# First convolution scored as plain fp32 products from a folded code table, first expert routing inside its turns

## The chip, the cores and the metric

The kernel runs on one NeuronCore of one Trainium2 chip. The metric is the device time of one execution in microseconds (us); each kernel is timed in several runs. The profile is one further execution, read by the hardware profiler. Its engines are PE (TensorE), DVE (VectorE), ACT (ScalarE), POOL (GpSimd) and SP (SyncE, which here only issues DMAs).

## The reference, cut to what matters

Sixteen images of 64 channels and 16 x 16 places pass through four blocks, each a "convolution" and an expert stage. Only the first convolution and what the first expert stage needs before it starts are changed:

```python
x = x + _L0_conv_ref(_ln_c(x), proj_w, proj_b, emb)      # _ln_c: mean and variance over the 64 channels
t = t + _L0_ffn_ref(_ln_t(t), ...)                       # 8 experts, the 2 likeliest of each token

# _L0_conv_ref, one row zf per token, K = 1024 codes of 64 values
zp = jnp.einsum('bchw,oc->bohw', z, proj_w) + proj_b[None, :, None, None]
dist = (zf * zf).sum(-1, keepdims=True) - 2.0 * (zf @ emb.T) + (emb * emb).sum(-1)[None, :]
idx = jnp.argmin(dist, axis=1)
z_q = emb[idx]
```

The first convolution thus gives each of the 4096 tokens the code nearest to its projected, normalised features. The term in zf alone is the same for all codes, so both kernels look for the largest of 2 z.e - e.e.

## The kernel before, in words

The program is written out by hand for each engine; semaphores order the engines and each engine does its work in the order written. `X` holds all tokens, 32 tiles of 128 tokens x 64 channels. The first convolution (`c0_*`) goes through eight turns (`PAIRS`), each for two images, that is four tiles j = 0 to 3 (`PT`).

*Preparation.* `load_first` brings the identity, the first images, the code table twice side by side, the projection and small tables. PE turns the 8 x 128 codes over (L251), ACT squares them (L266), and PE sums the squares with a matrix of -1 (L258). A product in plain fp32 is avoided: ACT and DVE split twice the code table into three bf16 parts `codes_a`, `codes_b`, `codes_c` (L267 to L291), and DVE splits the norms in three bf16 rows (`norm_parts`, L284 to L289).

*One turn g.* PE turns the images' channels into tokens (`c0_xload`, L299); DVE copies them to X (L421) and takes mean and variance (L122, L125); POOL makes the reciprocal deviation (L131, L132); DVE subtracts and multiplies (L136, L137); PE turns the normalised tokens (`c0_normt`, L306); ACT copies them to `xf` (L380), which has a 65th row of ones for the bias; PE projects them (`c0_project`, L313). ACT and DVE split the projection into three bf16 parts in `xa` and `xb` (L387 to L392, L457, L462). All of this is for the next turn's tokens and lies between the current turn's scorings. For each tile, `c0_scores` (L327) makes 128 x 1024 scores in two of four PSUM banks, by eight bf16 products: two with the norm rows, six with the parts. DVE finds the maximum (L471, eight values) and its index (L475). POOL gathers the code rows from memory (L526, an indirect DMA) and adds them to X (L535) one turn later. The two pairs of PSUM banks alternate by tile, so PE may score tile j+2 only when DVE has searched tile j (`c0_read`); a turn's first scoring also waits for the third part of the split (`c0_z`). DVE's index search of tile j waits until the gather of the same tile of the turn before has landed, since it overwrites the indices.

*Passage into the first expert stage.* The expert stages work on four blocks of eight tiles. `ffn_*_routing` gives the steps of one block: statistics (L920, L927), normalising on POOL (L1090 to L1103), turning the tokens (L707), the gate's logits (L715), ranking (L937 to L946), hits, combination (L950 to L980), turning the weights (L727, ACT L862), after which SP writes the weights to memory and reads them back broadcast (L672, L668). Block 0's steps stand before and in turn 7 and behind it; behind it DVE also takes the statistics of block 1; then comes `barrier` 1, where all four engines drain and wait for one another, and then the stage's products (up L773, activation on ACT L892, down L778). Behind some waits `wait_apart` increments a semaphore that nobody waits for.

## Time and profile before

| What | us |
|---|---|
| Three timed runs, median (lowest to highest) | 1025.54 (1020.04 to 1026.93) |
| Profiled execution: span, first to last instruction | 1015.0 |
| Profiled execution: its own device time | not recorded beside the span |
| PE busy in the span | 852.3 (84%) |
| DVE busy | 524.8 (52%) |
| ACT busy | 424.0 (42%) |
| POOL busy | 415.5 (41%) |
| Mean granted TensorE clock | 0.861 |

### The profile page before, as it was taken

What the parts mean: (1) busy time and instruction counts of PE and PEld (TensorE: products, weight loads), DVE (VectorE), ACT (ScalarE), POOL (GpSimd) and SP (SyncE); (2) the same over time, 40 slices, a digit from 0 to 9 for tenths busy, and PEclk for the clock granted to TensorE, in tenths of its full rate; (3) what the DMA queues carried; (4) which work ended last, traced back from release to release, by engine and by line L of the source; (5) the groups of instructions that cost most, each with busy time, mean ns of one, the idle gap of its engine ahead of it and who ended that gap; (6) DMA issues with size and microseconds to landing.
All of it is one profiled execution on the core that took longest, in us unless ns stands there. A gap on an engine that the chain in (4) does not pass through costs nothing.

```text
span 1015.0 us, 16664 instructions
## 1 busy us (share of the span) xinstructions
PE 852.3 (84%) x5582; PEld 395.5 (39%) x5588; DVE 524.8 (52%) x1845; ACT 424.0 (42%) x777; POOL 415.5 (41%) x533
## 2 busy tenths in 40 slices
PE   4768676889588999987778789989899998998995
PEld 1222222222355666665222478423333224652221
DVE  6887854555234444454553354355656453434542
ACT  3212213556235455454444343344344333646662
POOL 0343443555333233232343781544453643014642
PEclk9987777999559789799587785899999999969997
DMA  9410003222000000000234000422232310002341
GB/s 181 79 25 9 8 6 85 89 85 85 1 1 2 2 2 2 1 3 2 74 111 153 1 2 0 134 67 86 68 94 83 91 56 1 2 2 84 120 113 62
DMA packets 48701, 52.57 MB, mean 52 GB/s; under 512 B 18838, under 2 KB 27178, under 8 KB 48618
## 3 DMA queue, kind: packets, MB, share of 16 engines
q1 hardware_dynamic: 47594, 50.46, 18.0%
q0 software_dynamic: 1024, 1.05, 0.6%
q8 instruction: 46, 0.75, 0.3%
q14 instruction: 37, 0.30, 0.1%
HBM read 49.78 MB, written 1.70 MB: 51 GB/s over the span
## 4 chain that ended last, share of the span: by engine, by line
PE 62%; DVE 15%; issue 8%; POOL 8%; ACT 6%; POOLq 0%; SPq 0%; DVEq 0%; another core or an unknown queue 0%; DMA 0%; ACTq 0%
PE ps L773 17%; PE ps L778 11%; PE ps L1273 6%; PE ps L327 3%; DVE best L471 3%; DVE code L475 3%; PE ps L1245 2%; PE ps L1318 2%; PE ps L1268 2%; POOL work L1147 2%; PE ps L1644 2%; PE ps L715 2%; PE ps L1664 2%; DVE work L1009 1%; ACT work L892 1%
## 5 line engine op out<-in xcount | busy, mean ns | idle before, releaser
L773 PE MATMUL ps<-xT,wall 64*128 64x512 f32 x576 | 170.7, 674 | 5.7 <-ACT work L892 3.3
L778 PE MATMUL ps<-work,down 128*64 128x512 f32 x576 | 165.2, 655 | 6.8 <-POOL work L1135 6.1
L892 ACT ACTIVATE work<-ps,b1t 128x512 f32<-128x512 f32 x160 | 100.3, 685 | 79.2 <-PE ps L773 79.1
L1009 DVE TENSOR_TENSOR work<-aq,ps 128x512 f32<-128x512 f32 x128 | 82.2, 684 | 97.3 <-PE ps L773 89.5
L1128 POOL TENSOR_TENSOR work<-xT,cwb 128x512 f32<-128x512 f32 x64 | 81.4, 1275 | 104.0 <-PE ps L773 78.6
L887 ACT ACTIVATE aq<-ps 128x512 f32<-128x512 f32 x128 | 69.4, 594 | 118.9 <-PE ps L773 118.8
L1147 POOL TENSOR_TENSOR work<-work 128x512 f32<-128x512 f32 x56 | 71.0, 1268 | 81.6 <-DVE work L1035 79.3
L773 PEld LDWEIGHTS ps<-xT,wall 64*128 64x128 f32 x576 | 53.8, 203 | 111.8 <-issue 105.5
L1035 DVE SCALAR_TENSOR_TENSOR work<-ps,b1t,cwb 128x512 f32<-128x512 f32 x64 | 47.9, 748 | 77.7 <-PE ps L778 66.9
L773 PE MATMUL ps<-work,wall 64*128 64x512 f32 x256 | 73.5, 650 | 9.9 <-DVE work L1009 5.3
L1457 DVE TENSOR_REDUCE maxr<-ps 128x4 f32<-128x640 f32 x32 | 26.4, 825 | 79.6 <-PE ps L1273 79.6
L778 PEld LDWEIGHTS ps<-work,down 128*64 128x64 f32 x576 | 29.9, 140 | 94.2 <-DVE work L1009 35.1
L526 POOL DMA_INDIRECT zq<-in_L_conv_emb_dram,code x32 | 31.6, 988 | 69.2 <-DVE code L475 63.6
L327 PE MATMUL ps<-mt,ak 128*128 128x512 bf16 x186 | 57.6, 450 | 0.6 <-issue 0.4
L1392 ACT ACTIVATE pt<-ps 128x864 f32<-128x864 f32 x32 | 28.5, 891 | 63.5 <-PE ps L1273 63.5
L1268 PE MATMUL ps<-sight 32*128 32x160 bf16 (+2 forms) x512 | 38.0, 255 | 14.8 <-ACT pt L1393 7.7
L471 DVE MAX8 best<-ps 128x8 f32<-128x1024 f32 x32 | 39.3, 1228 | 17.8 <-PE ps L327 15.5
L773 PEld LDWEIGHTS ps<-work,wall 64*128 64x128 f32 x256 | 20.0, 189 | 62.6 <-POOL work L1128 38.1
L1273 PE MATMUL ps<-ak,aq 32*128 32x160 f32 (+2 forms) x512 | 43.4, 388 | 0.0
L475 DVE FIND_INDEX8 code<-best,ps 128x8 uint32<-128x1024 f32 x32 | 39.1, 1223 | 0.0
L1090 POOL TENSOR_SCALAR fveps<-fmv 128x8 f32<-128x8 f32 x16 | 3.6, 224 | 84.6 <-DVE fmv L927 61.4
L327 PE MATMUL ps<-norm_parts,ones 3*128 3x512 bf16 x64 | 22.5, 437 | 18.6 <-DVE ak L462 15.4
(245 smaller groups left out, 1484.1 us busy)
## 6 DMA issues: line engine op xcount, KB each, us to landing
cwb<-weight_rows SPq DMA_DIRECT2D x320, 128.0 KB, 3.0
wall<-in_L_ffn_w_dram SPq DMA_DIRECT2D x4, 512.0 KB, 10.6
wall<-in_L_ffn_W_dram SPq DMA_DIRECT2D x4, 256.0 KB, 9.5
out_dram<-tokens SPq DMA_DIRECT2D x8, 128.0 KB, 1.7
tokens<-in_x_dram SPq DMA_DIRECT2D x1, 896.0 KB, 5.3
ak<-in_L_conv_emb_dram SPq DMA_DIRECT2D x2, 256.0 KB
down<-in_L_ffn_W_dram SPq DMA_DIRECT2D x2, 256.0 KB
down<-in_L_ffn_w_dram SPq DMA_DIRECT2D x1, 512.0 KB
```

Of the source, the lines that this page charges most:

```text
L327: ins = pe.matmul(m.ps[:, 2 * (j % 2) + k, :], z, codes[:, k * 512:(k + 1) * 512], start=(n == 0), stop=(n == len(passes) - 1))
L471: n = o.step(dve.max(m.best[:, j, :], sc))
L475: dve.max_index(m.code[:, j, :], m.best[:, j, :], sc).then_inc(s.c0_read, 1)
L773: ins = pe.matmul(m.ps[:, bank + half, :], m.wall[r, at + g * P:at + (g + 1) * P], x[r, :], start=True, stop=True)
L778: ins = pe.matmul(m.ps[half * C:half * C + C, bank, :], m.down[l][:, n % G, :], m.hid[:, n % 3, half, :], start=start, stop=True, skip_gro ...
L887: act.activation(m.silu[:, n % 2, half, :], m.ps[:, 4 * (n % 2) + half, :], ACT.Silu).then_inc(s.f_silu, 1)
L892: act.activation(m.hid[:, n % 3, half, :], m.ps[:, 2 * (n % 2) + half, :], ACT.Gelu, bias=bias)\
L1009: dve.tensor_tensor(m.hid[:, n % 3, half, :], m.silu[:, n % 2, half, :], m.ps[:, 2 + half, :], ALU.mult)\
L1128: pool.tensor_tensor(m.xs[:, n % 2, :], m.xT[:, n // G, :], slot, ALU.mult).then_inc(s.f_pw, 1)
L1147: pool.tensor_tensor(acc, acc, m.part[:, k % 2, :], ALU.add).then_inc(s.f_pw, 1)
L1268: pe.matmul(m.ps[:, h, at_of(g, h):at_of(g, h) + w], m.place[r, g, t * P:(t + 1) * P], m.unseen[r, g, lo:lo + w], start=True, stop=True)
L1273: ins = pe.matmul(m.ps[:, h, at_of(g, h):at_of(g, h) + w], fixed[r, i % RING, g, t * P:(t + 1) * P], moving[r, i % RING, g, lo:lo + w], st ...
```

## The change

In the preparation the projection W, b is folded into the code table. `lead` is a 128 x 128 matrix with W in its first 64 columns, b in the 65th, and -0.5 at its lower half's 65th column. Multiplied with the turned codes over their squares (`codes_in`), it gives 65 rows that matter: W'e, and b.e - e.e/2. Doubled, they are `codes`, in fp32. A tile's scores are then two fp32 products of `xf` (64 feature rows, a row of ones, 63 rows of zeros, in two alternating buffers) with the halves of `codes`. The projection of each turn, the split into bf16 parts and the norm rows go.

The copy into X moves from DVE to ACT (`arrive`), subtracting the mean and multiplying from DVE to POOL (`norm`). Block 0's routing of the first expert stage is placed in pieces: statistics in turn 3, POOL's part in turns 3 and 4, the preparing transposes in turn 5, tokens and logits in turn 6, ranking, hits and combination between the searches of turn 7. The barrier between the first convolution and the first expert stage goes; PE instead waits for the last search, and the statistics of block sb wait for their additions. The memset of `vals` moves from the start to just before the first search. `wait_apart` is not used in the first convolution any more.

```diff
+        (m.lead[0:C, 0:C], d.L0_conv_proj_w),
+        (m.lead[0:C, C:C + 1], d.L0_conv_proj_b.rearrange("(o a) -> o a", a=1)),
     ]
     for dst, src in loads:
         sp.dma_start(dst, src, allow_slow_non_contiguous=src.shape[-1] == 1).then_inc(s.ld_first, 16)
@@ -158,7 +133,7 @@
     sp.dma_start(m.xall[:, 1:PAIRS, :], x[:, 1:PAIRS, :]).then_inc(s.c0_rest_in, 16)
...
+def c0_pe_fold(pe, nc, m, s):
+
+    pe.wait_ge(s.lead_set, 1)
     pe.wait_ge(s.codes_sq, 1)
-    pe.wait_ge(s.ones_rows, 1)
     for k in range(2):
-        ins = pe.matmul(m.ps[0:3, 2 + k, :], m.minus_one[0:C, 0:3], m.codes_sq[:, k * 512:(k + 1) * 512],
-                        start=True, stop=True)
+        ins = pe.matmul(m.ps[:, 2 + k, :], m.lead[:, :], m.codes_in[:, k * 512:(k + 1) * 512], start=True, stop=True)
     ins.then_inc(s.codes_n, 1)
 
...
+    act.activation(m.codes_in[C:P, :], turned[C:P, :], ACT.Square)
+    act.wait_ge(s.codes_plain, 1)
+    act.activation(m.codes_in[0:C, 512:CODES], turned[0:C, 512:CODES], ACT.Copy).then_inc(s.codes_sq, 1)
+
+
+def c0_act_codes(act, nc, m, s):
+    act.wait_ge(s.codes_n, 1)
+    act.activation(m.codes[:, 512:CODES], m.ps[:, 3, :], ACT.Copy, scale=2.0).then_inc(s.codes_ready, 1)
...
+    dve.tensor_copy(m.codes_in[0:C, 0:512], turned[0:C, 0:512]).then_inc(s.codes_plain, 1)
...
+    dve.tensor_scalar(m.codes[:, 0:512], m.ps[:, 2, :], 2.0, None, ALU.mult).then_inc(s.codes_ready, 1)
...
+    if g > 0:
+        pe.wait_ge(s.c0_here, g)
...
+    if g > 0:
+        pe.wait_ge(s.c0_xf, g)
...
-def c0_project(pe, m, s, g):
-
-    pe.wait_ge(s.c0_xf, g + 1)
-    pe.matmul(m.ps[:, 4, :], m.proj0[:, :], m.xf[:, :], start=True, stop=True).then_inc(s.c0_zp, 1)
...
-        pe.wait_ge(s.c0_z, g + 1)
+        pe.wait_ge(s.c0_xf, g + 1)
...
-    passes = ((m.ones3[:, :], m.norm_parts), (za, m.codes_a), (za, m.codes_b), (zb, m.codes_c))
-    for n, (z, codes) in enumerate(passes):
-        for k in range(2):
-            ins = pe.matmul(m.ps[:, 2 * (j % 2) + k, :], z, codes[:, k * 512:(k + 1) * 512],
-                            start=(n == 0), stop=(n == len(passes) - 1))
+    for k in range(2):
+        ins = pe.matmul(m.ps[:, 2 * (j % 2) + k, :], m.xf[:, g % 2, j * P:(j + 1) * P],
+                        m.codes[:, k * 512:(k + 1) * 512], start=True, stop=True)
     ins.then_inc(s.c0_scored, 1)
...
     c0_normt(pe, m, s, 0)
-    c0_project(pe, m, s, 0)
-    pe.wait_ge(s.c0_rest, 1)
     c0_xload(pe, m, s, 1)
-    pe.wait_ge(s.codes_ready, 1)
-
...
+    pe.wait_ge(s.codes_ready, 2)
+    tokens, logits, weights = ffn_pe_routing(pe, m, s, 0)
+
+    for g in range(PAIRS):
+        c0_scores(pe, m, s, g, 0)
+        if g + 1 < PAIRS:
             c0_normt(pe, m, s, g + 1)
-        c0_scores(pe, m, s, g, 1, b)
-        if ahead > 0:
-            c0_project(pe, m, s, g + 1)
...
+        if g == PAIRS - 2:
+            pe.wait_ge(s.prepared, 1)
+            tokens(0)
+        c0_scores(pe, m, s, g, 1)
+        if g + 2 < PAIRS:
             c0_xload(pe, m, s, g + 2)
...
+        c0_scores(pe, m, s, g, 2)
+        if g == PAIRS - 3:
+            prepare_pe(pe, nc, m, s)
+        elif g == PAIRS - 2:
+            pe.wait_ge(s.ld_up, 16 * UP_LOADS)
+            logits(0)
+        c0_scores(pe, m, s, g, 3)
     weights(0)
+    pe.wait_ge(s.c0_read, PAIRS * PT + 2)
...
+    def arrive(g):
+        x = m.X[:, g * PT:(g + 1) * PT, :]
+        act.wait_ge(s.c0_xt, g + 1)
+        act.activation(x.rearrange("p (a i) c -> p i a c", i=2),
+                       m.ps[:, 4, 0:2 * P].rearrange("p (i a c) -> p i a c", i=2, a=2), ACT.Copy).then_inc(s.c0_here, 1)
...
-        cols = slice(b * 512, b * 512 + 512)
-        act.wait_ge(s.c0_zp, g + 1)
-        act.activation(m.xa[:, cols], m.ps[:, 4, :], ACT.Copy).then_inc(s.c0_z1, 1)
-        act.wait_ge(s.c0_rest, g + 1)
-        act.activation(m.xb[0:C, cols], m.xa[0:C, cols], ACT.Copy).then_inc(s.c0_z1, 1)
-        act.activation(m.xb[C:P, cols], m.z_rest[C:P, :], ACT.Copy)
-        act.wait_ge(s.c0_z1, 2 * g + 2)
-        act.activation(m.xa[0:C, cols], m.z_rest[0:C, :], ACT.Copy).then_inc(s.c0_z2, 1)
-
...
+        if g > 1:
+            act.wait_ge(s.c0_scored, (g - 1) * PT)
+        act.activation(m.xf[0:C, g % 2, :], m.ps[0:C, 5, :], ACT.Copy).then_inc(s.c0_xf, 1)
+
+    arrive(0)
+    c0_act_first(act, nc, m, s)
+    c0_act_codes(act, nc, m, s)
...
+    features(0)
+    arrive(1)
+    tokens, exps, weights = ffn_act_routing(act, m, s, 0)
+    for g in range(PAIRS):
+        if g + 1 < PAIRS:
+            features(g + 1)
+        if g + 2 < PAIRS:
+            arrive(g + 2)
+        if g == PAIRS - 3:
             prepare_act(act, nc, m, s)
-        turn(2 * i + 2, 0)
-    tokens, exps, weights = ffn_act_routing(act, m, s, 0)
-    tokens(0)
+        elif g == PAIRS - 2:
+            tokens(0)
     exps(0)
...
+def c0_dve_stats(dve, o, m, s, g):
+
+    dve.wait_ge(s.c0_here, g + 1)
+    for j in range(PT):
+        ins = dve.bn_stats(m.stats[:, j, :], m.X[:, g * PT + j, :])
+    o.then(ins)
+    if g > 0:
+        dve.wait_ge(s.c0_xn, g)
+    for j in range(PT):
+        ins = dve.bn_aggr(m.mv[:, j, :], m.stats[:, j, :])
+    ins.then_inc(s.c0_mv, 1)
...
+    c0_dve_codes(dve, nc, m, s, o)
+    dve.sem_inc(s.c0_read, 2)
+    c0_dve_stats(dve, o, m, s, 1)
     o.then(dve.memset(m.vals[:, :, :, :, :], 0.0))
     ones = m.vals[:, :, :, :, :].rearrange("p a t g (h r) -> p (a t g h) r", r=32)
     dve.memset(ones[:, :, DEN], 1.0).then_inc(s.padded, 1)
-    dve.sem_inc(s.c0_read, 2)
...
-    def rest(g, b):
-        dve.wait_ge(s.c0_z1, 2 * g + 1)
-        dve.tensor_tensor(m.z_rest, m.ps[:, 4, :], m.xa[:, b * 512:b * 512 + 512], ALU.subtract).then_inc(s.c0_rest, 1)
-
-    def third(g, b):
-        dve.wait_ge(s.c0_z2, g + 1)
-        z3 = m.xb[C:P, b * 512:b * 512 + 512]
-        dve.tensor_tensor(z3, m.z_rest[C:P, :], z3, ALU.subtract).then_inc(s.c0_z, 1)
...
+    def argmax(g, j):
+        dve.wait_ge(s.c0_scored, g * PT + j + 1)
...
+        o.then(dve.max(m.best[:, j, :], sc))
+        if g > 0:
+            dve.wait_ge(s.c0_gathered[j], g * 16)
...
-    def turn(g, b, first=False, last=False):
-        c0_dve_norm(dve, o, m, s, g + 1, False)
-        argmax(g, 0, first)
-        argmax(g, 1, first)
-        rest(g + 1, 1 - b)
-        argmax(g, 2, first)
-        if not last:
-            c0_dve_arrive(dve, o, m, s, g + 2, False)
-        third(g + 1, 1 - b)
-        argmax(g, 3, first)
...
     stats, moments, rank, hits, combine = ffn_dve_routing(dve, m, s, 0)
-    dve.wait_ge(s.c0_added, 2)
-    stats(0)
-    moments(0)
-    turn(PAIRS - 2, 0, last=True)
-    for j in range(PT):
-        argmax(PAIRS - 1, j)
-    rank(0)
-    hits(0)
-    combine(0)
-    dve.wait_ge(s.c0_added, 4)
+    for g in range(PAIRS):
+        argmax(g, 0)
+        argmax(g, 1)
+        if g + 2 < PAIRS:
+            c0_dve_stats(dve, o, m, s, g + 2)
+        if g == 3:
+            stats(0)
+            moments(0)
+        elif g == PAIRS - 1:
+            rank(0)
+        argmax(g, 2)
+        if g == PAIRS - 1:
+            hits(0)
+            combine(0)
+        argmax(g, 3)
     stats(1)
     moments(1)
...
+    def norm(g):
+
+        x = m.X[:, g * PT:(g + 1) * PT, :]
+        pool.wait_ge(s.c0_mv, g + 1)
+        o.then(pool.tensor_scalar(m.veps[:, 0:PT], m.mv[:, 0:PT, 1], 1e-6, 1.0, ALU.add, ALU.mult))
+        o.then(pool.tensor_tensor(m.rstd[:, 0:PT], m.veps[:, 0:PT], m.minus_half[:, 0:PT], ALU.pow))
+        o.then(pool.tensor_tensor(m.xc[:, 0:PT, :], x, bcast(m.mv[:, 0:PT, 0:1], [P, PT, C]), ALU.subtract))
+        if g > 0:
+            pool.wait_ge(s.c0_nt, g)
+        pool.tensor_tensor(m.xn[:, 0:PT, :], m.xc[:, 0:PT, :], bcast(m.rstd[:, 0:PT].unsqueeze(2), [P, PT, C]),
+                           ALU.mult).then_inc(s.c0_xn, 1)
...
+    for g in range(PAIRS):
+        if g > 0:
             add(g - 1)
         gather(g, 0)
         gather(g, 1)
+        if g + 2 < PAIRS:
+            norm(g + 2)
         gather(g, 2)
-        if not last:
...
         if g == 3:
+            scale(0)
+        elif g == 4:
             weight_tables(pool, m, s, o)
...
+            centre(0)
+            spread(0)
     add(PAIRS - 1)
...
     def stats(sb):
+        if l == 0:
+            dve.wait_ge(s.c0_added, 2 * sb + 2)
...
```

Towards the end of the file, on each of the four engines (PE shown), with the later barriers renumbered:

```diff
             c0_pe(pe, nc, m, s)
+            ffn_pe(pe, nc, m, s, 0)
             barrier(pe, s, 1)
-            ffn_pe(pe, nc, m, s, 0)
...
```

The order of the instructions changes with it at three places. DVE in a turn of the middle, before; `xc` and `xn` are the normalising passes of the next turn, `aq` and `ak` the split of its projection, `best` and `code` the search:

```order
L136 TENSOR_TENSOR xc<-X,mv 128x256
L137 TENSOR_TENSOR xn<-xc,rstd 128x256
L471 MAX best<-ps 128x8
L475 MAX_INDEX code<-best,ps 128x8
L471 MAX best<-ps 128x8
L475 MAX_INDEX code<-best,ps 128x8
L457 TENSOR_TENSOR aq<-ps,ak 128x512
L471 MAX best<-ps 128x8
L475 MAX_INDEX code<-best,ps 128x8
L421 COPY X<-ps 128x2x2x64
L122 BN_STATS stats<-X 128x6 x4
L125 BN_AGGR mv<-stats 128x2 x4
```

and DVE now, from the third search of one turn to the statistics of the next:

```order
L398 MAX best<-ps 128x8
L401 MAX_INDEX code<-best,ps 128x8
L398 MAX best<-ps 128x8
L401 MAX_INDEX code<-best,ps 128x8
L398 MAX best<-ps 128x8
L401 MAX_INDEX code<-best,ps 128x8
L398 MAX best<-ps 128x8
L401 MAX_INDEX code<-best,ps 128x8
L362 BN_STATS stats<-X 128x6 x4
L367 BN_AGGR mv<-stats 128x2 x4
```

Beside its four searches DVE now has only the statistics in a turn; the copy, the passes and both subtractions are gone from it.

PE in the middle, before, from a turn's first scoring (two products with the norm rows, six with the parts) to its third:

```order
L327 MATMUL ps<-norm_parts,ones 128x512 x2
L327 MATMUL ps<-mt,ak 128x512 x6
L306 MATMUL ps<-ident,xn 64x128 x4
L327 MATMUL ps<-norm_parts,ones 128x512 x2
L327 MATMUL ps<-mt,ak 128x512 x6
L313 MATMUL ps<-xf,proj 128x512
L327 MATMUL ps<-norm_parts,ones 128x512 x2
L327 MATMUL ps<-mt,ak 128x512 x6
L299 MATMUL ps<-ident,tokens 128x128 x2
```

and now, over the same part of a turn (`mt` holds the folded code table):

```order
L289 MATMUL ps<-mt,xf 128x512 x6
L278 MATMUL ps<-ident,xn 64x128 x4
L289 MATMUL ps<-mt,xf 128x512 x2
L269 MATMUL ps<-ident,tokens 128x128 x2
L289 MATMUL ps<-mt,xf 128x512 x6
```

Eight products a tile have become two, the projection has gone, and the turning of the next images stands one scoring earlier. (The six of a row are the third and fourth tile of one turn and the first of the next.)

POOL in the middle now, where it had three gathers in a row and then only L131 and L132 of the norm; L459 are the additions to X, L450 the gathers:

```order
L459 TENSOR_TENSOR X<-X,zq 128x64 x4
L450 DMA zq<-in_L_conv_emb_dram,code 128x64 x2
L440 TENSOR_SCALAR veps<-mv 128x4
L441 TENSOR_TENSOR rstd<-veps,minus_half 128x4
L442 TENSOR_TENSOR xc<-X,mv 128x256
L445 TENSOR_TENSOR xn<-xc,rstd 128x256
L450 DMA zq<-in_L_conv_emb_dram,code 128x64 x2
```

The third and fourth gathers of a turn stand behind the whole norm of the pair after the next.

## Rows read from the trace of the kernel before

**Rows 1.** Busy us (instructions) by stretch, granted PE clock, DMA share, GB/s

```profile
57.15:71.73 14.58, 10.08 (x39) 3.45 (x40) 13.28 (x26) 3.08 (x5) 6.72 (x10) 0.95 0.11 28
71.73:88.00 16.27, 14.10 (x34) 4.27 (x34) 10.97 (x24) 3.08 (x5) 5.66 (x9) 0.52 0.04 7
140.00:148.00 8.00, 3.14 (x15) 1.05 (x14) 6.31 (x9) 0.00 (x0) 5.25 (x7) 1.00 0.04 8
```

**Rows 2.** Waits, 28 to 157 us: who waited for whom, us, times, longest

```profile
DVE best L471 <- PE ps L327: 15.5, 10, 5.0
PE ps L327 <- DVE ak L462: 15.4, 7, 2.6
```

**Rows 3.** Chain in order of time, to 180 us: start us, us, what

```profile
58.16 0.60 PE ps L306 x4
58.76 1.95 PE ps L327 x8
...
67.22 0.62 DVE stats L122 x4
...
68.38 0.69 DVE ak L462
...
73.78 3.63 PE ps L327 x8
```

**Rows 4.** Timeline of VectorE: start us, us, instruction [idle before]

```profile
138.92 1.23 DVE L471 MAX8 best<-ps 128x8 f32<-128x1024 f32 x1
...
141.54 1.21 DVE L471 MAX8 best<-ps 128x8 f32<-128x1024 f32 x1
```

**Rows 5.** Groups by line, 0 to 164 us: busy us, mean ns, idle before

```profile
L526 POOL DMA_INDIRECT zq<-in_L_conv_emb_dram,code x32 | 31.6, 988 | 69.2 <-DVE code L475 63.6 <-POOL X L535 5.0 <-issue 0.6
...
L535 POOL TENSOR_TENSOR X<-X,zq 128x64 f32<-128x64 f32 x32 | 9.6, 328 | 6.5 <-DMA zq<-in_L_conv_emb_dram,code 4.4 <-issue 1.9
L132 POOL TENSOR_TENSOR rstd<-veps,minus_half 128x4 f32<-128x4 f32 x8 | 8.3, 1038 | 0.7
...
L313 PEld LDWEIGHTS ps<-xf,proj 65*128 65x128 f32 x16 | 4.0, 260 | 2.8 <-ACT xf L380 1.1 <-issue 0.8
L131 POOL TENSOR_SCALAR veps<-mv 128x4 f32<-128x4 f32 x8 | 3.7, 463 | 25.7 <-DVE mv L125 25.3
...
L136 DVE TENSOR_TENSOR xc<-X,mv 128x256 f32<-128x256 f32 x8 | 3.3, 418 | 3.1 <-POOL rstd L132 3.1
...
L447 DVE MEMSET vals<- 128x2560 f32 x1 | 2.2, 2192 | 0.5 <-issue 0.5
```

**Rows 6.** Timeline: the start, and a projection at full clock

```profile
6.25 0.36 PE L249 MATMUL ps<-ident,nat 64*65 64x64 f32 x1 [2.18 <-DMA partsel<-in_partsel_dram]
...
8.61 1.28 ACT L266 ACT_TABLE_LOAD   x1 [8.61 <-PE ps L251]
...
10.97 3.57 PE L258 MATMUL ps<-pt,minus_one 64*3 64x512 f32 x4 [2.45 <-ACT pt L266]
...
29.18 1.23 DVE L471 MAX8 best<-ps 128x8 f32<-128x1024 f32 x1
...
60.53 1.02 PE L313 MATMUL ps<-xf,proj 65*128 65x512 f32 x2
```

**Rows 7.** Two lines: duration ns min/median/max, first and last start

```profile
L1541 POOL TENSOR_TENSOR xc<-X,mv x16: 400/402/402, 256.7 to 432.2; 128x128 f32<-128x128 f32 x16
...
L1095 POOL TENSOR_TENSOR fxc<-X,fmv x16: 1043/1048/1053, 145.5 to 962.5; 128x512 f32<-128x512 f32 x16
```

**Rows 8.** Timelines of VectorE and PE at the end of the scoring

```profile
157.02 0.20 DVE L937 TENSOR_TENSOR lg<-ps,gate_b 128x64 f32<-128x64 f32 x1
...
161.25 1.10 DVE L920 BATCH_NORM_STATS2 fstats<-X 128x6 f32<-128x64 f32 x8
...
163.14 3.79 PE L773 MATMUL ps<-xT,wall 64*128 64x512 f32 x8 [0.72 <-DVEq L102]
...
170.02 1.97 PE L778 MATMUL ps<-work,down 128*64 128x512 f32 x4
```

246 lines of the change are left out of this document (57 added, 189 removed), and 2 rows, old and new, of the table SEMS.

## Prediction

> **What bounds the kernel now.** I read the page first, then the busy time by stretch, the waits of the first 157 us, the chain in order of time, and the timelines of the start and of the passage into the first expert stage. The change touches nothing behind that passage, so everything is about the first 163 us of a span of 1015.0 us. In the stretches, one scoring turn (four tiles of 128 tokens) takes 14.58 us at nearly full TensorE clock with VectorE busy 13.28 us of it, and 16.27 us once the granted clock is down to 0.52, with PE busy 14.10 us [rows 1]. So at full clock VectorE sets the turn, at half clock TensorE. The waits say how the two hang together: PE waited 15.4 us in 7 waits, up to 2.6 us each, for VectorE's third part of the split projection (`ak`, L462), and VectorE waited 15.5 us for scores [rows 2]. The chain shows the same order in a full-clock turn: transposes 0.60 us, scores 1.95 us, statistics, L462, then the next maximum [rows 3]. The clock fell behind a PE wait of that kind: the chain has L462 at 68.38 us and the scores at half clock from 73.78 us (3.63 us against 1.95) [rows 3].
>
> **The turn afterwards, at full clock.** One search of maximum and index repeats every 2.61 us when nothing is late (138.92 to 141.54 us with its scores ready, 2.62) [rows 4]; four are 10.5 us. VectorE loses the copy into X, the two normalising passes (418 ns each by L136 [rows 5]) and the two subtractions of the split (L457 and L462, 0.69 us for the latter [rows 3]), and keeps the statistics: 67.22 to 68.38 us [rows 3], 1.2 us with its gap. That is 10.5 + 1.2 = 11.7 us in place of 14.58.
>
> PE must have a tile's scores within a search. It issues two fp32 products of 128x512. The trace of before has no pair of them at full clock. Bounds: two lone ones as L313 at 60.53 us, 2 x 1.02 = 2.04 us [rows 6], and half of the half-clock pair L258, 3.57 / 2 = 1.8 us [rows 6]. I take 1.95 us, which is also what the eight bf16 products take now [rows 3], so PE's scoring itself gets no cheaper and no dearer; only the projection (1.02 us a turn) goes. With an allowance of 0.3 us for the hand-over on both sides 1.95 fits into 2.61. The four transposes of the normalised tokens (0.60 us [rows 3]) stand in front of a turn's second scoring and do not quite fit: I charge 0.25 us a turn (0.60 less the 0.36 us that 1.95 and 0.3 leave of 2.61), 2 us over eight; the extra PE work placed in turns 5 and 6 (the preparing transposes, tokens, logits) 1 us more. Bounds of this term: 0 and 8 x 0.6 + 3 = 8 us.
>
> GpSimd takes over the two normalising passes. The trace has no 128x256 pass there; 128x128 takes 402 ns and 128x512 1048 ns [rows 7], so I take 0.62 us each and keep 0.40 and 1.05 as ends. A turn on GpSimd is then 4 gathers at 0.99 us, four additions at 0.33 us with the 0.2 us a gather that precedes them idle (6.5 us over 32), the power and the scale 1.04 and 0.46 us (L526, L535, L132, L131 [rows 5]), passes 1.24 us: 8.8 us, 9.7 at the dear end, under 11.7. Queued behind the norm of pair g+2 on GpSimd are gathers 2 and 3 of pair g. Who waits for those are VectorE's index searches one turn later (their wait on the gathered tile), 11 us away. So this edit costs nothing on the path; if the cover went, it would cost its excess over 11.7 us in each turn. The copy into X (0.4 us) goes to ScalarE, which also loses five passes a turn.
>
> **A page against this.** By rows, a 128x512 pass costs GpSimd 1048 ns [rows 7], and the 128x256 pass costs VectorE 418 ns [rows 5]. The Trainium skill (GPSIMD Engine Reference, Performance versus the Vector engine) says elementwise arithmetic runs roughly twice as slowly on GpSimd and advises VectorE for it. Twice 418 ns would be 0.84 us, an estimate between my ends; the sum would stay as it is, and only the GpSimd rival below would gain.
>
> **The start.** The first search starts at 29.18 us; on the way stand the last load's landing (PE L249 at 6.25), ScalarE's table load behind the turned codes (8.61, 1.28 us), the norms and their three-way split on VectorE, and the split of the first projection [rows 6]. Afterwards: codes turned by 8.0 us (one load fewer; 6.25 stays the late bound, 8.5). ScalarE's table load is now done at about 5.4, because its first work is the copy into X. Square of 64x1024 and copy of 64x512 1.6 us: 9.7. The fold is again two fp32 products, cold as L258 [rows 6], 3.57 us: 13.3. Halves of the code table out of PSUM 0.7 us, beside them the transposes of the normalised pair: 14.3. Features copied: 14.9, first scores from 15.0, 17 to 18.6 when done. But VectorE is not free: statistics of pair 1 need X, which ScalarE copies only at 15.2, so until 16.6, and then the memset of `vals` (2192 ns [rows 5]), which formerly lay in idle time ahead of everything, until 19.0. First search at 19.2 us: 10.0 us earlier. Bounds: 17.5 (memset hidden) and 22. Pair 1 is normalised on GpSimd by 19.5 at best, so the second tile's scores are late once: 1.5 us.
>
> **The end.** The routing of the first expert block stands now after the last search: VectorE L937 at 157.02 us until the next statistics at 161.25 us, 4.2 us, then block 1's statistics (1.10 us) and moments, and the first up-projection at 163.14 us behind the barrier, 1.9 us after those statistics began [rows 8]. Afterwards the 4.2 us lie between the last two searches and the 1.8 us of block 0's statistics in turn 3; both remain VectorE time, so I count them in full. Gone from the path are the statistics of block 1 and the barrier (1.9 us together), since PE needs only the last read of the scores. The first stage also opens cold now: 163.14 to the first down-projection at 170.02 us, 6.9 us [rows 8]. With PE warm, two units of up-projection take 2.3 us, and table load and two activations decide: 1.1 + 1.3 + 1.3 + the third unit's 1.1 = 4.8 us. That is 2.1 us gained (bounds 0 and 3; the broadcast weights come about when they are needed).
>
> **The sum.** 32 searches x 2.61 = 83.5; six statistics x 1.2 = 7.2; block statistics 1.8; ranking to weights 4.2; late second tile 1.5; PE lateness 3. Together 101.2 us from 19.2 us: the last read ends at 120.4 us, the up-projection starts at 120.5 us where it was 163.14: 42.6 us. With 2.1 us at the opening 44.7 us. Of these, 10 us are the start, about 2.6 us x 8 = 21 us the lighter turn, the rest the half-clock turns and the passage. The profiled execution's span becomes 1015.0 - 44.7 = 970.3 us. Around it lie 10.5 us to the median 1025.54 of the runs (5.0 us to the fastest, 1020.04; the page gives no time of its own for that execution beyond the span), so 980.8 us.
>
> **Rivals.**
> 1. *The clock falls again in the scoring.* For it: PE will pause some 0.6 us in every tile, and it fell at 70 us although PE had been busy 10.1 us of 14.6 [rows 1]. Against it: that fall came behind a wait of 2.6 us, and from 140 to 148 us the grant stayed 1.00 with PE busy only 3.14 us [rows 1]; the new order has no wait above 1 us after turn 0, and at half clock PE is never idle, which is when it rose before. Price: half-clock tiles cost 3.57 us, so a turn is PE's, 4 x 3.57 + 1.8 (six transposes at twice the 0.15 us each of the four in 0.60 us [rows 3]) = 16.1 us, 4.2 us over 11.9. All eight: 34 us, time 1015. Half of them: 998. The Trainium skill (TensorE: Matmul & The Clock Gate, A second HAM failure mode) describes just this, PE pausing briefly between groups as it cycles through PSUM banks, with the clock swinging between its levels. By that rule this rival is the outcome; the 140 to 148 us row speaks for the other. Chance 0.20, three quarters of it partial.
> 2. *GpSimd sets the turn.* If passes, gathers and additions hold each other up (the small scale operation takes 463 ns on average, L131 [rows 5]) to 13 us a turn, VectorE waits for X or normalised tokens: 8 x 1.2 = 10 us, time 991. Against it is the sum of 8.8 us. Chance 0.12.
> [...] PE-bound, the last read is at about 36 + 32 x 4.61 = 183.5 us (36: start 15, transposes 13, extras and routing tail 8), 20 us later than 163.14: time 1046. It decides from 3.98 us a tile on. Against it: both half-clock conditions are needed together, and L258 ran four records in 3.57 us. Chance 0.02.
> 4. *The change does not do what it says*, for instance the searches wait each turn for the features and the turn stays near 14 us: only start and passage are won, about 1003. Chance 0.02.
>
> **Numbers.** My forecast, VectorE-bound turns near 11.7 us at full clock, has 0.64: 981 us, its own range 972 to 989. The range 970 to 1003 takes in the GpSimd rival, partial half clock and the bounds of start, PE lateness and passage. One per cent, 10 us, is what a measurement of this kernel can tell from no change; faster by more than that 0.93, within it 0.05 (all turns at half clock with something lost behind it), slower 0.02.
>
> **What would show it.** The first search near 19 us; searches 2.6 us apart with under 0.3 us idle, and turns of 11.7 to 12 us; scores of two fp32 products in 1.9 to 2.0 us; PE clock 0.95 or more between 20 and 120 us; GpSimd passes near 0.6 us; the first up-projection at 120 us with the first down-projection 5 us behind. Wrong it is if scores take 3.6 us over several turns (rival 1), if VectorE's idle time ends on GpSimd (rival 2), or if the expert stage behind grows by what was won.

## The result and the profile after

The changed kernel takes 957.63 us (median of four runs, 954.36 to 961.36), the kernel before beside it 1022.79 us (four runs, 1017.04 to 1026.93): a ratio of 0.938, 95% interval 0.931 to 0.944. The prediction was 981.0 us, its range 970 to 1003: the direction and the mechanism came out, the time lies 12 us below the range. The profiled execution after has a span of 959.5 us and took 961.36 us itself, so 1.9 us lie around the span; the profiled execution of before, span 1015.0 us, took 1017.04.

Where the 55.5 us between the two spans arose (starts of stages in the two traces, before and after):

| Point | before | after | gained so far |
|---|---|---|---|
| first search | 29.18 | 19.79 | 9.4 |
| end of the last search | 157.1 | 115.7 | 41.4 |
| first up-projection | 163.14 | 115.79 | 47.4 |
| first down-projection | 170.02 | 121.01 | 49.0 |
| second convolution's first product | 261.31 | 210.61 | 50.7 |
| the stage after it | 488.07 | 432.43 | 55.6 |

Behind that the two traces run in step to within 2 us. The last 4.9 us arose in the second convolution, whose code the change leaves alone; experiment 1 looks at them. The medians differ by 65.2 us, 9.7 more than the spans: the profiled execution of before lies 5.8 us under the median of its four runs, that of after 3.7 above its own, and 0.2 is what lies around the spans.

Busy time by stretch of the kernel after (us, then busy us and instructions of PE, PE's weight loads, DVE, ACT, POOL; granted clock; DMA share; GB/s), for turns 1, 3 and 6, to set beside [rows 1]:

```profile
30.53:41.28 10.75, 8.25 (x20) 2.99 (x18) 10.58 (x21) 0.98 (x2) 6.20 (x11) 1.00 0.59 127
52.40:66.29 13.89, 10.00 (x22) 3.87 (x21) 12.32 (x38) 0.97 (x2) 8.89 (x15) 0.88 0.18 35
87.85:101.59 13.74, 10.92 (x32) 5.66 (x32) 9.84 (x14) 1.19 (x2) 7.65 (x12) 0.88 0.07 12
```

A turn is 10.75 us where it was 14.58, with VectorE busy for 10.58 of it and the clock at 1.00. Two turns are not like that, and in both PE ran partly at half clock. The waits from 20 to 116 us (who, for whom, us, times, longest), beside [rows 2]:

```profile
PE ps L289 <- DVE code L401: 16.2, 19, 3.1
DVE best L398 <- PE ps L289: 5.4, 3, 3.8
PE ps L278 <- POOL xn L445: 4.9, 3, 2.1
```

VectorE's wait for scores has shrunk from 15.5 us in ten waits to 5.4 in three, and what PE waits for is mostly VectorE's search of the tile two before (16.2 us in 19 waits). Groups by line, to 116 us, beside [rows 5]:

```profile
L401 DVE FIND_INDEX8 code<-best,ps 128x8 uint32<-128x1024 f32 x32 | 39.2, 1224 | 0.0
L398 DVE MAX8 best<-ps 128x8 f32<-128x1024 f32 x32 | 38.8, 1213 | 5.5 <-PE ps L289 5.4
...
L442 POOL TENSOR_TENSOR xc<-X,mv 128x256 f32<-128x256 f32 x8 | 4.9, 615 | 0.6
```

GpSimd's pass of 128x256 takes 615 ns: I had taken 0.62 us, between 0.40 and 1.05. The start and the passage, from the timelines of all engines (start us, us, instruction, idle before), beside [rows 6] and [rows 8]:

```profile
0.73 1.28 ACT L329 ACT_TABLE_LOAD   x1 [0.73 <-PEq L2301]
...
10.40 3.75 PE L235 MATMUL ps<-codes_in,lead 128*128 128x512 f32 x4 [1.80 <-ACT codes_in L244]
...
15.77 1.96 PE L289 MATMUL ps<-mt,xf 128*128 128x512 f32 x4 [0.57 <-issue]
...
17.47 2.19 DVE L391 MEMSET vals<- 128x2560 f32 x1 [0.48 <-issue]
19.79 1.17 DVE L398 MAX8 best<-ps 128x8 f32<-128x1024 f32 x1
...
114.51 1.22 DVE L401 FIND_INDEX8 code<-best,ps 128x8 uint32<-128x1024 f32 x1
115.79 5.29 PE L683 MATMUL ps<-xT,wall 64*128 64x512 f32 x12 [1.88 <-DVE code L401]
...
121.01 1.08 PE L688 MATMUL ps<-work,down 128*64 128x512 f32 x4
```

The fold is cold as forecast (3.75 us), the first pair of fp32 products takes 1.96 us (forecast 1.95), the memset of `vals` holds the first search back to 19.79 (forecast 19.2), and the up-projection starts 0.06 us behind the last index search. Two timelines show what the odd turns lost. Turn 3, PE and then VectorE:

```profile
62.60 3.65 PE L289 MATMUL ps<-mt,xf 128*128 128x512 f32 x4 [3.15 <-DVE code L401]
...
58.25 1.07 DVE L832 BATCH_NORM_STATS2 fstats<-X 128x6 f32<-128x64 f32 x8
59.36 0.64 DVE L839 BATCH_NORM_AGGREGATE fmv<-fstats 128x2 f32<-128x6 f32 x8
...
66.29 1.23 DVE L398 MAX8 best<-ps 128x8 f32<-128x1024 f32 x1 [1.37 <-PE ps L289]
```

While VectorE takes the block's statistics PE idles 3.15 us, its next scores run at half clock (3.65 us), and VectorE waits 1.37 us for them. Turn 6:

```profile
89.66 0.86 PE L278 MATMUL ps<-ident,xn 128*64 128x128 f32 x4 [2.09 <-POOL xn L445]
90.32 1.06 PE L617 MATMUL ps<-ident,fxn 128*128 128x128 f32 x4
91.17 4.67 PE L289 MATMUL ps<-mt,xf 128*128 128x512 f32 x8
...
94.16 1.23 DVE L398 MAX8 best<-ps 128x8 f32<-128x1024 f32 x1 [3.76 <-PE ps L289]
```

GpSimd is late with the normalised tokens, because centring and spreading for the expert stage stood in front of them; PE waits 2.09 us for it, runs at half clock, turns the expert stage's tokens too, and VectorE stands for 3.76 us.

### The profile page after: what moved, and what is told of

Same layout as the page of the kernel before. It is cut to its first block, busy times and chain, and to the rows that moved or that the text cites. A ratio compares the mean times of both kernels' runs of the same rounds, so it can differ in the third digit from the quotient of the medians.

```text
span 959.5 us, 16206 instructions
## 1 busy us (share of the span) xinstructions
PE 816.7 (85%) x5443; PEld 388.9 (41%) x5443; DVE 497.1 (52%) x1800; ACT 404.8 (42%) x750; POOL 422.8 (44%) x549
## 3 DMA queue, kind: packets, MB, share of 16 engines
q0 software_dynamic: 1024, 1.05, 0.6%
## 4 chain that ended last, share of the span: by engine, by line
PE 61%; DVE 13%; POOL 10%; issue 8%; ACT 5%; DMA 1%; POOLq 1%; SPq 0%; DVEq 0%; ACTq 0%
PE ps L683 18%; PE ps L688 12%; PE ps L1185 6%; DVE best L398 3%; DVE code L401 2%; PE ps L1230 2%; PE ps L1157 2%; PE ps L1180 2%; POOL work L1059 2%; PE ps L625 2%; PE ps L1556 2%; PE ps L1576 2%; DVE work L921 1%; PE ps L1774 1%; ACT work L802 1%
## 5 line engine op out<-in xcount | busy, mean ns | idle before, releaser
L289 PE MATMUL ps<-mt,xf 128*128 128x512 f32 x128 | 65.2, 635 | 17.0 <-DVE code L401 16.2
L450 POOL DMA_INDIRECT zq<-in_L_conv_emb_dram,code x32 | 31.6, 987 | 27.5 <-DVE code L401 22.3
L289 PEld LDWEIGHTS ps<-mt,xf 128*128 128x128 f32 x128 | 22.8, 198 | 48.4 <-issue 34.5
L398 DVE MAX8 best<-ps 128x8 f32<-128x1024 f32 x32 | 38.8, 1213 | 5.5 <-PE ps L289 5.4
L1185 PE MATMUL ps<-ak,aq 32*128 32x160 f32 (+2 forms) x512 | 40.8, 370 | 0.0
```

What stands on the lines that cost most here:

```text
L289: ins = pe.matmul(m.ps[:, 2 * (j % 2) + k, :], m.xf[:, g % 2, j * P:(j + 1) * P], m.codes[:, k * 512:(k + 1) * 512], start=True, stop=True)
L398: o.then(dve.max(m.best[:, j, :], sc))
L1185: ins = pe.matmul(m.ps[:, h, at_of(g, h):at_of(g, h) + w], fixed[r, i % RING, g, t * P:(t + 1) * P], moving[r, i % RING, g, lo:lo + w], st ...
```

## The experiments

All with the same inputs, in groups on one chip; "up" is the start of the first up-projection in the profiled execution. That row and the search's period answer most questions better than the time does, since the later stages scatter (first run).

**1. The changed kernel again, twice** (`a0_again`, `a0_third`).

> The changed kernel itself once more, for its spread. Theory A (the gain ends at the first expert stage; what the second convolution gained in the first profile, 4.9 us, is the granted clock of that one execution): the start of the second convolution's first transposes is again near 210.7 us, give or take 2, and the stretch from there to the second expert stage lies anywhere between 219 and 229 us. Rival B (the second convolution is faster because of the change): it is again near 221.8 us. Time near 958 us.

> The changed kernel itself, beside the two others. Its scoring should be as in the two executions before: first search at 19.8 us, first up-projection at 115 to 116 us, second convolution from 210.5 us. Its time, 955 to 970 us, should differ from run to run by what the second and third convolution take at a higher or lower clock.

Measured: 967.41 us (951.01 to 972.19) and 952.33 us (944.82 to 967.32). Up at 115.22 and 113.44 us; in `a0_third` the clock stayed up behind the late tokens of turn 6, and VectorE stood for 2.06 us there and not for 3.76. The second convolution, unchanged code, in the traces of before, after and `a0_third` (same columns; the edges lie within 0.15 us of the stage's own):

```profile
261.31:488.07 226.76, 195.49 (x2681) 132.62 (x2681) 103.49 (x407) 103.33 (x228) 68.99 (x126) 0.82 0.01 2
```

```profile
210.74:432.56 221.82, 190.12 (x2681) 130.19 (x2682) 103.46 (x409) 103.20 (x228) 68.86 (x126) 0.84 0.01 2
```

```profile
208.05:422.86 214.81, 181.71 (x2681) 125.06 (x2682) 103.39 (x408) 102.84 (x228) 68.82 (x126) 0.88 0.01 2
```

VectorE, ScalarE and GpSimd do the same work in all three; the stage is as long as the clock makes it, 227 us at 0.82 and 215 at 0.88. Whether the 4.9 us between the first two are chance is not shown. `a0_again` took 221.8 us there (210.43 to 432.25 us), the very number of rival B, and `a0_third` 214.8, which fits neither. The other kernels of this study leave the stage alone too. From its first product to the up-projection behind it the five profiled executions with the old scoring took 221.7 to 228.5 us, four of them over 228; the twelve with the new one took 212.6 to 229.7 us, three of them about 228 or more. So the new scoring does not make the stage short each time, but it may meet a higher clock there more often; that stays open.

A larger scatter sits in the third convolution: 69.6 us at a clock of 0.70 in the changed kernel's first trace, 81.8 us at 0.56 in `a0_again`. All twelve times of the changed kernel lie between 944.8 and 972.2 us, median 957.6. A difference of a few us between two kernels has to be read from the trace.

**2. `wait_apart` back, and taken from before** (`e1_apart`: the changed kernel; `e2_before_no_apart`: the kernel before).

```diff
-        dve.wait_ge(s.c0_scored, g * PT + j + 1)
+        wait_apart(dve, m, s.c0_scored, g * PT + j + 1)
...
-            dve.wait_ge(s.c0_gathered[j], g * 16)
+            wait_apart(dve, m, s.c0_gathered[j], g * 16)
```

> The changed kernel with wait_apart back on the two waits of each search of VectorE. Theory A: the gap between maximum and index search (0.03 us now, 0.17 us before) and the search's period (2.46 us now, 2.61 before) are those of before again: 31 x 0.15 = 4.7 us, the first up-projection at about 120.5 us instead of 115.8, time 5 us up. Rival C (the search is shorter because the split's passes no longer share PSUM and SBUF with it): period stays 2.46 us, time stays.

> The kernel before with one thing changed: the search no longer uses wait_apart behind its two waits. Theory A (the extra increment behind a wait lengthens every search): searches with their scores ready repeat every 2.46 us instead of 2.61, a full-clock turn shrinks by 0.6 us, and the first up-projection comes up to 4 us earlier (159 to 163 us; less where TensorE at half clock sets the turn). Theory B (the shorter period of the changed kernel came from its other edits, such as the lighter GpSimd or the missing passes): the period stays at 2.61 us and the up-projection at 163.

Timeline of VectorE in `e1_apart`:

```profile
38.96 1.21 DVE L398 MAX8 best<-ps 128x8 f32<-128x1024 f32 x1
40.35 0.09 DVE L401 MATCH_VALUE_LOAD code<-best,ps 128x8 f32 x1 [0.18 <-DVE best L398]
...
41.57 1.21 DVE L398 MAX8 best<-ps 128x8 f32<-128x1024 f32 x1
```

The period is 2.61 us again, with the 0.18 us between maximum and index search back; in the changed kernel it is 2.47 (maxima at 49.93 and 52.40 us). Yet up came at 115.36 us, not 4.7 us later: no scores ran at half clock before it, and VectorE waited 1.51 us for scores in turn 6 and not at all in turn 3, where the changed kernel has 3.76 and 1.37. In the kernel before, taking it out shortened a search to 2.49 us and brought up from 163.14 to 153.53 us, more than twice the 4 us of theory A. Full-clock turns became 14.05 us (14.58); the rest goes with the clock, which was 0.95 from 44 to 116 us and 0.83 in before (experiment 6). Time: 1009.58 us against 1019.03, ratio 0.986 (0.980 to 0.992). `e1_apart` took 971.04 us (948.44 to 976.96). The size per search is thus shown in both kernels; its effect on the end depends on what the clock does.

**3. The passage** (`e3_barrier`: `barrier` 1 back ahead of the expert stage; `e4_routing_behind`: also block 0's routing back behind the last search, its statistics behind turn 5's last search, GpSimd's part to turn 7).

> The changed kernel with a barrier of all engines back between first convolution and first expert stage. GpSimd's last addition ended at 120.1 us and the statistics of block 1 at 117.4 us, PE's first up-projection started at 115.8: with the barrier it starts at about 120.8, 5 us later. Theory A: the whole 5 us stay, less what the next block's tokens (PE at 125.2) give back: time 3 to 5 us up. Rival D (the first expert stage takes it back, since its GpSimd and DMA work was waiting anyway): time up by under 1 us.

> The scoring as changed, but block 0's routing placed as before (statistics behind turn 5, GpSimd's part ahead of its last turn, tokens in turn 7, logits, ranking, hits and weights behind the last search) and the barrier back. Theory A: the placement and the barrier together are worth the ranking chain on three engines (4.2 us of VectorE, 1 us of logits, 1 us of weights), 2 us of barrier and some 3 us of turn 7 waiting for the tokens: 8 to 12 us up, and the fp32 scoring with its lighter turns keeps the other 40 us. Rival E (half of the gain is the placement): 20 us or more up.

The up-projections, from PE's timelines of `e3_barrier` and `e4_routing_behind`:

```profile
119.59 3.57 PE L683 MATMUL ps<-xT,wall 64*128 64x512 f32 x8 [6.45 <-POOLq L102]
```

```profile
117.02 3.78 PE L679 MATMUL ps<-xT,wall 64*128 64x512 f32 x8 [0.72 <-DVEq L102]
```

With the barrier 4.85 us lie between the last search's end (114.74) and up (119.59), where the changed kernel has 0.06: as expected. The first expert stage did not take it back, the second convolution's first product came at 215.37 us (210.61). The time, 970.23 us (969.92 to 970.34), is 2.8 us above `a0_again` beside it, which is within the scatter. With the routing behind the scoring, up comes only 1.2 us later than in the changed kernel, not 8 to 12: the last search ends at 110.9 us, since turns 3 and 6 are not disturbed as before (turn 7 is: VectorE waits 4.1 us there behind the expert stage's tokens), and the routing and barrier take 6.1 us after it. Time 968.97 us (955.36 to 970.12). So placing the routing inside the turns moved VectorE's 4.2 us without saving them, and what it saved of the rest it largely lost in turns 3 and 6. The two runs side by side say it more sharply, for both have the barrier: with the routing inside the turns up came 2.6 us later, in one execution of each. A kernel with the routing behind the scoring and no barrier was not run.

**4. The normalising passes back on VectorE** (`e5_norm_on_dve`).

```diff
+        if g + 1 < PAIRS:
+            c0_dve_norm(dve, o, m, s, g + 1)
         argmax(g, 0)
```

> The changed kernel with the two normalising passes (subtract, multiply) back on VectorE ahead of a turn's first search; GpSimd keeps scale and power only. Theory A (VectorE sets the turn, so every pass taken from it shortens the turn by its own length): a turn grows by the two passes, 2 x 0.42 us and two hand-overs, 0.9 to 1.2 us, seven times, so the first up-projection comes 6 to 8 us later than 115.8 us, at 122 to 124. Part comes back in turn 6, where PE waited 2 us for GpSimd's pass. Theory B (the passes would lie beside something else, and their move was worth nothing): up-projection at 116 to 118 us.

```profile
43.91 0.41 DVE L374 TENSOR_TENSOR xc<-X,mv 128x256 f32<-128x256 f32 x1
44.34 0.42 DVE L377 TENSOR_TENSOR xn<-xc,rstd 128x256 f32<-128x256 f32 x1
44.69 1.23 DVE L409 MAX8 best<-ps 128x8 f32<-128x1024 f32 x1
```

VectorE now spends 0.8 us ahead of each turn's first search, seven times; up came at 119.06 us, 3.3 us later. That lies between the numbers of the two theories: 5.8 us were added (7 x 0.83) and 0.5 at the start, and 3.3 came back in turn 6, where GpSimd was no longer late (3.0 us from one maximum to the next where the changed kernel has 6.3). By turn it is theory A (11.63 us from 29.81 to 41.44, against 10.75); the part coming back was larger than I had allowed. 967.24 us (964.47 to 971.99).

**5. The kind and the amount of products** (`e6_bf16_four`, `e7_bf16_one`).

```diff
-    for k in range(2):
-        ins = pe.matmul(m.ps[:, 2 * (j % 2) + k, :], m.xf[:, g % 2, j * P:(j + 1) * P],
-                        m.codes[:, k * 512:(k + 1) * 512], start=True, stop=True)
+    for n in range(4):
+        for k in range(2):
+            ins = pe.matmul(m.ps[:, 2 * (j % 2) + k, :], m.xf[:, g % 2, j * P:(j + 1) * P],
+                            m.codes[:, k * 512:(k + 1) * 512], start=(n == 0), stop=(n == 3))
...
-        m.xf = sb("xf", [P, 2, 512])
+        m.xf = sb("xf", [P, 2, 512], BF16)
```

> The changed kernel with the features and the folded table rounded to bf16 and every tile scored by eight bf16 products of 128x512 in place of two in fp32 (the same product four times over, summed), so PE is as long busy with a tile, 1.95 us. Theory A (only PE's time and its waits matter, for the turn and for the clock): search period 2.46 us, clock as in the changed kernel, half clock for 0 to 10 us of the scoring, first up-projection at 114 to 118 us. Theory B (bf16 products let the clock fall more easily than fp32 products in the same places): half clock for over 20 us of the scoring, as in the kernel before, and the up-projection at 120 us or later.

> The changed kernel with features and folded table in bf16 and only two bf16 products a tile, PE busy with a tile a quarter as long, about 0.5 us at full clock and 1 us at half (the scores are coarser than the reference's). Theory A (VectorE sets the turn with PE hidden): the period stays at 2.46 us, and since even half-clock scores fit into it, the clock costs nothing in the scoring; the up-projection comes at 110 to 114 us. Theory B (PE's time of a tile stands on the path between two searches): period under 2.4 us, up-projection under 108 us.

Busy time by stretch, 24 to 64 us, of `e6_bf16_four` and then of `e7_bf16_one`:

```profile
24.00:64.00 40.00, 28.22 (x129) 12.24 (x132) 39.33 (x91) 2.92 (x6) 27.36 (x42) 1.00 0.41 73
```

```profile
24.00:64.00 40.00, 18.53 (x49) 6.01 (x50) 39.35 (x91) 3.01 (x7) 27.40 (x42) 0.50 0.41 73
```

Eight bf16 products give the same picture as two in fp32: clock 1.00, VectorE 39.3 of 40 us busy, up at 114.05. With two bf16 products the clock stays at its lower level for nearly the whole scoring, PE is 46% busy, and VectorE is as busy as before: the period stays 2.46 us and up comes at 112.43. So in this order VectorE alone sets the turn, and neither the fp32 format nor the clock is what makes it short, as long as a tile's products end within a search (1.03 us at half clock here). Times 950.59 us (948.94 to 959.18) and 950.27 (943.64 to 955.33); the first owes part of that to a second convolution of 211 us. Both kernels score with bf16 features and codes, coarser than the changed kernel does.

**6. What made the clock fall in the kernel before** (`e8_before_warm`, `e11_before_fp32`, `e12_before_filled`).

```diff
+def fill(pe, m, n):
+    for k in range(n):
+        pe.matmul(m.ps[:, 7, :], m.codes_a[:, 0:P], m.codes_a[:, 0:512], start=True, stop=True)
```

`e8_before_warm` has it with n = 6 ahead of the wait for `c0_z` only; `e12_before_filled` also with 6 at the head of `c0_normt` and 2 ahead of each fourth tile.

> The kernel before, with six products of 128x512 in bf16 on PE ahead of the wait for the third part of the split in turns 1 to 5 (their result is read by nobody). It tests what made the clock fall in the scoring of before, where 37.5 us ran at half clock. [...]
> The kernel before with every tile's eight bf16 products replaced by two in fp32 over the same bytes read as fp32 (scores that mean nothing; every engine's other work, order and waits as before), 1.96 us of PE a tile as now. Together with the changed kernel on bf16 products it separates the kind of product from the order around it. Theory A (the waits and the order make the clock fall): half clock for some 30 to 40 us of the scoring as before, first up-projection at 160 to 165 us. Theory B (fp32 products keep the clock up where bf16 products do not): under 10 us at half clock, turns near 14.6 us throughout, up-projection at 150 to 155 us.

> The kernel before with bf16 products (read by nobody) ahead of each of PE's three waits in a turn of the middle: six ahead of the normalised tokens, two ahead of the fourth tile, six ahead of the third part of the split. [...] Theory B (the clock of this scoring falls whatever PE does in its waits): 30 us or more at half clock again, and the up-projection at 166 us or later, since the fillers also cost at half clock.

The same stretch, 44 to 116 us, in before, `e8_before_warm`, `e11_before_fp32`, `e12_before_filled` and, from experiment 2, `e2_before_no_apart`, in this order:

```profile
44.00:116.00 72.00, 54.65 (x183) 18.16 (x186) 59.41 (x108) 15.38 (x25) 31.20 (x50) 0.83 0.08 16
```

```profile
44.00:116.00 72.00, 58.72 (x202) 20.16 (x200) 58.22 (x107) 13.49 (x22) 30.04 (x49) 0.83 0.07 15
```

```profile
44.00:116.00 72.00, 49.73 (x128) 20.48 (x127) 65.96 (x126) 16.87 (x35) 34.21 (x53) 0.93 0.08 16
```

```profile
44.00:116.00 72.00, 61.28 (x265) 23.20 (x268) 65.69 (x124) 16.88 (x35) 34.06 (x53) 1.00 0.09 17
```

```profile
44.00:116.00 72.00, 51.13 (x205) 17.83 (x203) 66.08 (x131) 16.87 (x35) 33.80 (x54) 0.95 0.08 17
```

Filling part of one wait (2.4 to 2.6 us before) changed nothing: clock 0.83 again, up at 166.56 us, theory B by the letter. The waits of 1.3 to 1.6 us for the normalised tokens had stayed, and 1.1 to 1.7 us of those for `ak`. Filling all of them, so that none was over 0.9 us, kept the clock at 1.00 throughout, and it fell at the place where the fillers end (turn 6):

```profile
115.02 0.60 PE L336 MATMUL ps<-norm_parts,ones 3*128 3x512 bf16 x2 [1.60 <-DVE ak L471]
115.55 2.22 PE L336 MATMUL ps<-mt,ak 128*128 128x512 bf16 x6
120.39 1.03 PE L312 MATMUL ps<-ident,xn 128*64 128x128 f32 x4 [2.62 <-DVE xn L137]
```

Up came at 158.30 us (163.14), later than the 152 to 156 of theory A because turns 6 and 7 then ran low; the time is 1000.78 us against 1023.09 (ratio 0.978, 0.973 to 0.983), a larger gain than the 4.8 us of the up-projection, and no trace says where the rest lies. With fp32 products in place of the bf16 ones and everything else as before, the clock is 0.93 there and up at 152.12, between the two theories; the falls are shorter, but waits of 2.2 to 2.8 us are there (1004.85 us, 996.66 to 1005.8, against 1021.85). That is no evidence for fp32: with bf16 products and only `wait_apart` gone the clock was 0.95 in the same stretch, with five waits for `ak` of up to 2.4 us. Nor is it known how far 0.83 itself scatters, since the kernel before was profiled once. Why such a wait is followed by a fall in one turn and not in the next stays open: `e1_apart` had one of 3.30 us in turn 3 and no fall. What is shown is that PE's waits matter: with all of them filled there was no fall, and one came as soon as the fillers ended.

**7. The pieces placed otherwise** (`e9_pieces`, `e10_pieces_warm`, `e13_vals_early`).

```diff
-        if g == PAIRS - 2:
-            pe.wait_ge(s.prepared, 1)
-            tokens(0)
...
         elif g == PAIRS - 2:
+            pe.wait_ge(s.prepared, 1)
+            tokens(0)
+        c0_scores(pe, m, s, g, 3)
...
+        if g == PAIRS - 1:
+            rank(0)
+            hits(0)
+        argmax(g, 2)
         if g == 3:
             stats(0)
-            moments(0)
         elif g == PAIRS - 1:
-            rank(0)
-        argmax(g, 2)
-        if g == PAIRS - 1:
-            hits(0)
             combine(0)
         argmax(g, 3)
+        if g == 3:
+            moments(0)
...
+            centre(0)
         elif g == 4:
             weight_tables(pool, m, s, o)
-            centre(0)
+        elif g == 5:
             spread(0)
```

> The changed kernel with its pieces moved: the second pair of images gets a load of its own, and its turning, copy and statistics come ahead of the fold, as does the memset of vals; block 0's statistics and moments lie around the last search of turn 3 instead of both before the third; centring in turn 3, spreading in turn 5 instead of both in turn 4; tokens and logits one scoring later in turn 6. Theory A (in the changed kernel VectorE waited for PE because of these pieces, 3 us behind the memset and statistics, 3 to 4 us in turn 3, 3.8 us in turn 6 behind GpSimd's centring and spreading): first search at 17.8 us, no half clock between 20 and 110 us, gaps of over 4 us between searches only where statistics or ranking fill them, first up-projection at 108 to 110 us where it was 115.8. Theory B (the clock falls whatever the placement): half-clock scores again, up-projection 112 us or later. The whole: 950 to 960 us, if the later stages do not move.

> As the kernel with its pieces moved, and PE turns the identity over 18 times between its first three steps (read by nobody), so that it is not idle before the fold. Theory A (the fold took 3.75 us because the clock was at 1.2 GHz behind PE's waits): the fold takes about 2 us, the first search starts 1.5 us earlier, at 16.2 us, and the up-projection follows it. Theory B (the clock rises only later, or the extra products delay the turning of the codes): fold still 3.6 us, first search at 17.8 us or up to 1 us later.

> As the kernel with moved pieces and PE kept busy ahead of the fold, but the memset of vals (2.2 us) stands right behind the first pair's statistics, in VectorE's wait for the turned codes. Theory A (in the run before, the fast fold ended at 11.9 us, and the memset that VectorE was in until 13.8 us held back the first half of the code table): the code table is copied at 12 us, the first scores start at 12.9 us and take 1.96 us, the first search starts at 15.0 us and the up-projection at 106 us. Theory B (the clock falls again ahead of the first scores, as at 14.6 us there, whatever the memset does): first search at 16.5 us or later.

Two stretches of `e9_pieces`, and from its timeline the first scores and the first up-projection:

```profile
24.00:64.00 40.00, 30.22 (x80) 12.29 (x80) 39.37 (x84) 3.89 (x8) 28.16 (x43) 1.00 0.41 75
64.00:104.00 40.00, 29.95 (x85) 12.54 (x85) 38.81 (x89) 3.94 (x15) 26.48 (x44) 1.00 0.06 12
```

```profile
14.91 1.96 PE L290 MATMUL ps<-mt,xf 128*128 128x512 f32 x4 [0.79 <-DVE mt L261]
...
107.83 5.09 PE L686 MATMUL ps<-xT,wall 64*128 64x512 f32 x12 [1.50 <-DVE code L402]
```

The clock is at 1.00 from 24 to 104 us, VectorE is busy 38.8 of 40 us where the changed kernel had 34.35 in the second stretch, and up comes at 107.83 us in place of 115.79: theory A in each of its points, the first search at 16.91 us even earlier than its 17.8. 951.37 us (942.96 to 961.52).

Keeping PE busy ahead of the fold did make the fold short, and won nothing, in two ways. `e10_pieces_warm`:

```profile
9.95 1.95 PE L236 MATMUL ps<-codes_in,lead 128*128 128x512 f32 x4 [1.15 <-ACT codes_in L245]
...
14.63 3.63 PE L290 MATMUL ps<-mt,xf 128*128 128x512 f32 x4 [2.29 <-DVE mt L261]
```

The fold ended at 11.9 us, but VectorE was in its memset of `vals` until 13.8 us; PE waited 2.29 us for the table's half, and then its first scores ran at half clock. First search 18.30 us, up 109.27, 949.21 us (930.85 to 960.0). `e13_vals_early`, with the memset ahead:

```profile
7.08 2.19 DVE L388 MEMSET vals<- 128x2560 f32 x1 [0.48 <-issue]
9.31 0.68 DVE L256 COPY codes_in<-ps 64x512 f32<-64x512 f32 x1
...
10.76 3.28 PE L236 MATMUL ps<-codes_in,lead 128*128 128x512 f32 x4 [1.94 <-ACT codes_in L245]
```

The memset now held back VectorE's copy of the turned codes to 9.31 us (8.18 in the run before), PE waited 1.94 us for it and the fold was mostly cold again: first search 17.62 us, up 108.58, theory B's side. 949.53 us (947.74 to 953.32).

The three kernels with moved pieces together have a median of 950.6 us over twelve runs, the changed kernel 957.6 over its twelve. The 7 us fit the 8.0 us of the up-projection, but the two sets of times overlap, and the bf16 kernels of experiment 5, with up 3.2 to 6.2 us later, have the same medians: it is the trace that shows the gain. Theirs are the earliest up-projections of this study.

## Why the prediction was right, and where it was wrong

**The steps that failed.** The forecast took 44.7 us off, all of them ahead of the first down-projection. The spans differ by 55.5 us and the medians by 65.2. Three steps of the text carry the miss:

- "Around it lie 10.5 us to the median 1025.54 of the runs". I took the difference between the profiled span and the median for something that lies around every execution. In every profiled execution here it is 1.8 to 2.0 us; the profiled execution of before was simply the quickest of its four (1017.04 us). The term was 8.6 us too large.
- "One search of maximum and index repeats every 2.61 us", used for the time afterwards. It was read correctly from [rows 4], and the diff said that `wait_apart` goes; I did not connect the two, and costed that edit at nothing without saying so. Measured: 2.47 us. Experiment 2 shows the size, 0.12 to 0.14 us a search; 4.5 us over 32.
- "The change touches nothing behind that passage, so everything is about the first 163 us". What lies behind was put at nothing. Between the first down-projection and the end of the second convolution the spans gained 6.6 us more, 1.7 in the expert stage and 4.9 in the second convolution at a higher clock. Why the latter is open (experiment 1).

Forecast span and measured span differ by 10.8 us (970.3 and 959.5), the first step adds 8.6, and the profiled execution after is 3.7 us above its median: 23.1 of the 23.4 us between 981.0 and 957.6. No one of the three accounts for the miss alone. With 1.9 in place of 10.5 the forecast is 972.2 us and the lower end of its range 961, still above the measured 957.6. Nor is 1.9 a sound base for a median: it hopes that the next profiled execution is as quick among its runs as this one was, and it was not. Put on the median of before, 1022.79 us, the gain of 44.7 us gives 978.1, so that 20.5 us are missing: 10.8 in the two traces, 9.7 in where the two profiled executions lie among their runs. In which stages those 9.7 us lie no trace shows.

**The terms of the sum**, from the first search to the last read:

| Term | forecast | measured | why |
|---|---|---|---|
| first search | 19.2 | 19.79 | the memset of `vals`, as described |
| 32 searches | 83.5 | 79.0 | 2.47 us each, not 2.61 |
| six statistics | 7.2 | 5.6 | 0.93 us each (3.39 less 2.46) |
| block statistics | 1.8 | 1.7 | |
| ranking to weights | 4.2 | 4.2 | |
| late second tile | 1.5 | 0 | scores ready within the period |
| PE lateness | 3 | 5.4 | 0.2 in turn 2, 1.4 in turn 3, 3.8 in turn 6 |
| last read | 120.4 | 115.7 | |

The largest miss in this table is the search.

**Right by its mechanism.** VectorE sets the turn (experiments 4 and 5): of the 3.8 us that a full-clock turn lost, 0.5 are `wait_apart` and 0.8 the two passes; the other 2.5 are the copy, the two subtractions and the waits for the split, not separated further. fp32 pairs at 1.96 us, GpSimd's pass at 0.615, the fold, the memset and the passage all came within 0.6 us. First up to first down took 5.2 us (forecast 4.8).

**PE lateness** was put in a general allowance of 0.25 us a turn for the transposes; those cost 0.24 us once, in turn 2. What was late were the two turns in which pieces of the routing stand, which I had costed only as VectorE time: the statistics as an idle PE in turn 3, and GpSimd's 3 us of tables, centring and spreading as late tokens in turn 6.

**The rivals.** The clock (rival 1) fell at two places, for 1.4 us and part of 3.8, and not in whole turns. Its condition was misjudged: "no wait above 1 us after turn 0" was to speak against it, but PE waited 1.48 us in each turn, 3.15 in turn 3 and 2.09 in turn 6, and the clock held behind the first kind. Its price of 4.2 us a turn was not tested, since no run has a whole turn of fp32 products at half clock; experiment 5 adds that a low clock costs nothing where a tile's products still fit in a search. GpSimd (rival 2) did set one turn, though the sum of its work, 6.2 us of 10.75, is far from a bound: it was late through one row of pieces in the wrong place. The Trainium skill (TensorE: Matmul & The Clock Gate, A second HAM failure mode) would have had the clock swing under PE's brief pauses between PSUM banks; with pauses of 0.5 us and one of 1.5 us a turn it stayed at 1.00 in turn 1, and from 24 to 104 us of `e9_pieces`. Under the longer pauses of the kernel before it did swing (0.83), and filling the pauses stopped it (experiment 6): there the section describes what happened.

**Where the 47 us at the up-projection are from**: 9.4 the start, 6.0 the passage, 32 the scoring. (Putting the passage back costs only 1.2 us, experiment 3: the scoring then loses less to its pieces, which cost VectorE 5.1 us of waiting in turns 3 and 6.) Of the 32, the old kernel gives 9.6 when only `wait_apart` goes, 4.8 when PE's waits are filled up to turn 5, and 11 with another kind of product and no other work changed. So part of its loss was the clock and not VectorE's work; how large a part in a usual execution is not shown, with one profile of the kernel before.

## What to carry to other kernels

Compare like with like: span with span, or median with median. Know the profiled execution's own time and how far one kernel's runs lie apart before a span is turned into a median. Where an engine sets the pace by a small repeated step, every instruction between two such steps counts, a semaphore increment too: 0.14 us by 32. Work put "inside" a loop is not free: see what the other engines wait for while it runs, spread it so that no wait exceeds the usual one, and check each engine's row of pieces, not only its sum.

## What the runs showed of the hardware

The granted clock fell where PE had waited, but not behind every wait. From 44 to 116 us the kernel before had 0.83 with waits up to 2.6 us, and 0.83 still with waits of 1.1 to 1.7 us twice a turn although PE was busier, 1.00 with none above 0.9 us; without `wait_apart` it had 0.95 with waits up to 2.4 us. In the changed kernel it was 1.00 in turns with a single wait of 1.5 us and others of 0.5; a wait of 3.15 us was followed by a fall in its three traces, one of 3.30 us in `e1_apart` was not. Whether the format of the products matters for it is open: in the new order it made no difference, and the 0.93 of fp32 products in the old one lies beside 0.95 with bf16. Two fp32 products of 128x512 take as long as eight in bf16 (1.96 and 1.89 us). With a semaphore increment of its own behind the wait between maximum and index search, the gap between them is 0.17 to 0.18 us where it is 0.03 without (`e1_apart`); one search takes 0.12 to 0.14 us more.
